# Zero products behind the units of maxima ahead of the first exponentials

## What is computed

```python
q = (x @ Wq).reshape(B, S, 2 * H, d).transpose(0, 2, 1, 3) * scaling     # 32 sub-heads, d = 4
k = (x @ Wk).reshape(B, S, 2 * H, d).transpose(0, 2, 1, 3)
v = (x @ Wv).reshape(B, S, H, 2 * d).transpose(0, 2, 1, 3)
scores = jnp.where(causal_mask, -jnp.inf, jnp.einsum('bhqd,bhkd->bhqk', q, k))
probs = jax.nn.softmax(scores, axis=-1).reshape(B, H, 2, S, S)
attn = jnp.einsum('bhqk,bhkd->bhqd', probs[:, :, 0] - lam * probs[:, :, 1], v)
attn = attn * rsqrt(mean(attn * attn) + eps) * rms_w * (1 - LAMBDA_INIT)
x = layernorm(x + attn.transpose(0, 2, 1, 3).reshape(B, S, H * 2 * d) @ Wo)
r, k = sigmoid(xr @ W_r), xk @ W_k          # xr, xk: x mixed with the token before
out = layernorm(x + r * (square(relu(k)) @ W_v))
```

## Time and profile before

| | |
|---|---|
| Median of 3 runs | 441.94 us (440.62 to 442.19) |
| Profiled execution, whole | 441.16 us |
| Its span in the profile | 439.4 us |
| TensorE busy | 395.6 us, 90% |
| VectorE busy | 397.3 us, 90% |
| ScalarE busy | 350.9 us, 80% |
| GpSimd busy | 225.2 us, 51% |
| TensorE clock granted, mean | 0.965 of full speed |

### The profile page before, as it was taken

One profiled execution on the slowest core, in us unless ns is written; L12 is line 12 of the kernel. 1 busy time (PEld: TensorE's weight loads), 2 busy tenths in 40 slices (PEclk: granted clock), 3 DMA queues, 4 the chain that ended last, 5 costly groups with the idle time before them and its releaser, 6 DMA issues.

```text
span 439.4 us, 16522 instructions
## 1 busy us (share of the span) xinstructions
PE 395.6 (90%) x5720; PEld 186.5 (42%) x5721; DVE 397.3 (90%) x565; ACT 350.9 (80%) x732; POOL 225.2 (51%) x514
## 2 busy tenths in 40 slices
PE   5846999999999999999999999999999999999882
PEld 3512444444444444444444444444444444445552
DVE  1889999999999999999999999999999999773854
ACT  2520799999999999999999999999999999787143
POOL 7300132565656565656565656565656565558412
PEclk9975599999999999999999999999999999999998
DMA  5564254321121111111111111111111110000011
GB/s 141 177 215 145 90 194 148 98 51 51 51 53 48 48 48 48 48 48 48 48 48 49 48 48 49 48 48 48 48 48 48 48 50 28 26 3 1 1 49 48
DMA packets 21390, 28.44 MB, mean 65 GB/s; under 512 B 4960, under 2 KB 9952, under 8 KB 21232
## 3 DMA queue, kind: packets, MB, share of 16 engines
q1 hardware_dynamic: 20768, 27.58, 20.9%
q10 hardware_dynamic: 592, 0.46, 0.3%
HBM read 20.39 MB, written 9.47 MB: 68 GB/s over the span
## 4 chain that ended last, share of the span: by engine, by line
PE 60%; DVE 13%; ACT 12%; issue 9%; DMA 2%; SPq 1%; POOL 1%; ACTq 1%; DVEq 0%; POOLq 0%
PE acc L677 26%; PE mx L595 13%; DVE part_max L1133 10%; ACT e_buf L1028 10%; PE ex L647 8%; PE ex L685 3%; PE mx L604 2%; PE ex L631 1%; SPq L316 1%; DMA x_tok<-in_L_attn_x 1%; PE mx L814 1%; PE mx L769 1%; PE mx L677 1%; PE ex L696 1%; POOL rs L545 1%
## 5 line engine op out<-in xcount | busy, mean ns | idle before, releaser
L1133 DVE TENSOR_REDUCE part_max<-mx 128x2 f32<-128x1024 f32 (+2 forms) x288 | 334.8, 1211 | 6.3 <-PE mx L595 2.3
L1028 ACT ACTIVATE e_buf<-ex 128x512 f32<-128x512 f32 x576 | 306.2, 601 | 36.5 <-PE ex L647 30.7
L516 POOL TENSOR_SCALAR_AFFINE_SELECT e_buf<-e_buf 128x256 f32<-128x256 f32 x256 | 100.7, 411 | 168.9 <-ACT e_buf L1028 168.7
L677 PE MATMUL acc<-e_buf,v_grp 128*32 128x256 f32 x2756 | 181.5, 352 | 4.1 <-issue 2.5
L647 PE MATMUL ex<-qe,ke 26*128 26x512 bf16 (+3 forms) x768 | 144.7, 333 | 0.7 <-ACT e_buf L1028 0.6
L595 PE MATMUL mx<-km,qm 29*128 29x128 bf16 (+3 forms) x1280 | 116.9, 270 | 12.8 <-DVE part_max L1133 10.0
L595 PEld LDWEIGHTS mx<-km,qm 26*128 26x128 bf16 (+1 forms) x1280 | 41.7, 93 | 113.8 <-DVE part_max L1133 73.5
L677 PEld LDWEIGHTS acc<-e_buf,v_grp 128*32 128x32 f32 x2756 | 64.8, 109 | 55.8 <-issue 35.5
L647 PEld LDWEIGHTS ex<-qe,ke 26*128 26x128 bf16 x768 | 45.4, 91 | 20.7 <-ACT e_buf L1028 8.2
L499 POOL TENSOR_TENSOR r_rms<-sq_eps,minus_half 128x16 f32<-128x16 f32 x15 | 43.7, 2912 | 0.1
L604 PE MATMUL mx<-mask,pick 32*128 32x128 bf16 x512 | 25.8, 220 | 0.0
(11 more groups left out here) (137 smaller groups left out, 253.6 us busy)
## 6 DMA issues: line engine op xcount, KB each, us to landing
qm<-q_rows SPq DMA_DIRECT2D x32, 128.0 KB, 2.5
km<-k_rows SPq DMA_DIRECT2D x32, 128.0 KB, 2.7
qe<-q_rows SPq DMA_DIRECT2D x32, 128.0 KB, 2.5
ke<-k_rows SPq DMA_DIRECT2D x32, 128.0 KB, 2.7
q_rows<-part_q SPq DMA_DIRECT2D x6, 256.0 KB, 3.0
k_rows<-part_k SPq DMA_DIRECT2D x6, 256.0 KB, 3.3
q_rows<-part_q SPq DMA_DIRECT2D x6, 192.0 KB
k_rows<-part_k SPq DMA_DIRECT2D x6, 192.0 KB
```

The costliest lines, as they stand in the source:

```text
L516: pool.affine_select(out=e, in_=e, compare_op=ALU.is_ge, fill=0.0, base=0, pattern=[[0, PAIR], [1, P]], channel_multiplier=-1)\
L677: last = pe.matmul(out, v, e, start=first, stop=over, skip_group_check=True)
L1028: nc.scalar.activation(e_buf[:, b, i, :], ex[:, ex_slot(b, i) % EX_BANKS, :], ACT.Exp).then_inc(s["exped"], 1)
L1133: nc.vector.tensor_reduce(target, mx_of(n, pr, m)[:].rearrange("p s (a b) -> p s a b", a=a), AX.X, ALU.max).then_inc(s["maxed"], 1)
```

## The change

`keep_busy` is defined ahead of the first loop and takes the bank as an argument. In that loop it is called with two products after the weights' transposes behind unit 4, and with two products behind each of the units 5 to 15. That makes 12 calls and 24 products of 512 columns, into bank 0 of `ex`. In unit 12 they stand ahead of the turn of the maxima, which keeps bank 2. The two calls at the end are as before. No wait, no DMA and no instruction of another engine is added, moved or removed.

```diff
+            def keep_busy(count, bank):
+                for i in range(count):
+                    pe.matmul(ex[:, bank, :], identb[:], mask_zero[:].rearrange("p c t -> p (c t)"), start=True,
+                              stop=True, skip_group_check=True)
+
...
                 if u == 4:
                     pe.wait_ge(s["rest_done"], 2 * NCH)
                     turn_weights()
+                    keep_busy(2, 0)
+                if u > 4:
+                    keep_busy(2, 0)
                 if u == NU + 3:
                     turn_maxima(0, 2)
...
-            def keep_busy(count):
-                for i in range(count):
-                    pe.matmul(ex[:, 2, :], identb[:], mask_zero[:].rearrange("p c t -> p (c t)"), start=True,
-                              stop=True, skip_group_check=True)
-
             turn_sums(NPAIR + 1, 0, last_acc)
-            keep_busy(14)
+            keep_busy(14, 2)
...
-            keep_busy(10)
+            keep_busy(10, 2)
```

## The result

The changed kernel is slower. It took 447.30 us on the median (446.79 to 448.62) against 442.06 (440.62 to 442.37) before; the ratio is 1.0129, with a 95% interval of 1.0114 to 1.0144. The forecast was 441.1 us, in a range up to 443.2. The profiled execution took 448.62 us, with a span of 446.9.

The account below looks back on a forecast made before the run. VectorE's reductions were taken to bound the kernel up to about 44 us, with TensorE's low clock lengthening pair 0 behind that. Terms: -1.71 us won in pair 0, +0.9 delay, sum -0.8, from 441.94 to 441.1 us; range 439.4 to 443.2.

Parts of the forecast that it names:

- What the low clock costs: Low clock costs nothing up to about 44 us; pair 0 at full clock would run like pair 2, winning 1.71 us.
- The high end of the gain: Pair 0 shortened to VectorE's own work of 10.75 us, winning 1.99 us.
- rival (c): Early clock rise and pair 0 at VectorE's bound: -1.9 us, 440.0 us; chance 0.12.
- When the clock rises: Clock rises at 37.0 us, within unit 9, after 7.6 us of busy TensorE; delay until then 0.9 us.
- The price of a step: At the low clock a unit and its two zero products keep TensorE 1.29 us, where VectorE needs 1.13.
- the estimated 0.11 us a load: Weight loads not hiding behind the zero products: delay about 1.1 us longer, sum an estimated +0.3 us; set aside.
- Rival (b): Zeros don't raise the clock; TensorE bounds until unit 15, 2.75 us late, nothing won: 444.7 us; chance 0.08.
- Rival (a): Clock rises, then falls in pair 0's first bursts; 0.25 us won, delay 0.9 stays: +0.65, 442.6 us; chance 0.18.
- Scatter: Allowance of 0.6 us to either side for run-to-run spread, as the three earlier runs lie 1.6 us apart.

Follow-up runs that it names:

- r9: r7 with four zero products instead of two behind units 2 and 3, and two behind the scores of pair 0's first four bursts: 439.38 us, ratio 0.9948.
- r5: Changed kernel with 14 zero products in one run behind unit 4 instead of two: 446.15 us, ratio 1.0106.
- r12: r5 with its run of 14 broken up, seven products over 128 rows and seven over rows 0 to 63 in turn: 454.64 us, ratio 1.0303.
- r13: Changed kernel with four zero products behind each unit instead of two: 444.59 us, ratio 1.0073.
- r7: Changed kernel with eight zero products while TensorE waits for the first rows, and two behind every unit from the first on: 442.09 us, ratio 1.0029.
- r4: Changed kernel with one zero product behind each unit instead of two: 442.22 us, ratio 1.0015.
- r11: Changed kernel with its 24 zero products over rows 0 to 63 alone, which the units leave free: 447.64 us, ratio 1.0125.
- r8: Kernel before the change, without its 24 zero products near the end: 444.24 us, ratio 1.0051.
- r6: r5 with all 38 products of real numbers instead of zeros: 446.01 us, ratio 1.0088.
- r1: Changed kernel with real numbers as both weights and moving data of the 24 products: median 446.49 us.
- r2: Changed kernel with real moving data in the 24 products, weights still the identity: median 444.89 us.
- r3: Changed kernel with real weights in the 24 products, zeros still streaming: median 446.92 us.
- r10: Changed kernel once more, nothing altered, for its scatter: twelve executions from 441.19 to 448.95 us, median 446.91.

## Why the prediction was wrong

**What the low clock costs, right.** Up to 44 us nothing, in pair 0 the difference to a steady pair: 1.71 us. r9 has 12.74 - 11.08 = 1.66, and its span is 437.8 against 439.4, 1.6 less. That VectorE's own work is the other bound was right (11.02 busy of 11.08), but its size was not: I took 10.75 from pair 2, where VectorE has 13 instructions, and pair 0 has 16. The high end of the gain was 12.74 - 11.02 = 1.72, not 1.99, and rival (c), built on the 10.75, asked for more than pair 0 can give.

**When the clock rises, wrong.** This is the step that failed. I took the 7.6 us of a busy TensorE ahead of the only rise in the trace for what a rise takes, and put it behind 29.34. The changed kernel's TensorE was busy for 18.3 us (31.5 to 49.8) with no rise, and the clock came up at 58.8, not at 37.0; by the mean clocks 12 of 16 executions went that way. The busy column counts a product until its end, and so covers the 0.11 us in which no columns stream; r5 and r12 have it alike and part at the clock. I had also argued that the work would be denser than that of 46.40 to 54.01. It was not: I had not looked at the starts, 0.54 apart where 0.43 is the time of the columns. Whether that is why the clock stayed low is open, as said under r13: in r7's profile the same pattern brought it up.

**The price of a step, too small.** 1.29 us was 1.50. I took the step of the zeros from the end of the kernel, where one follows another, and used it for changes between units and zeros, which have no row there. The missing 0.21 are the two changes. r4 shows that the loss is this step: with one product behind each unit it is 1.08, under VectorE's 1.13, and nearly all of the loss is gone. The Trainium skill, "TensorE: Matmul & The Clock Gate", section "Part 3: Packing small matmuls", would have given about this sum, by the estimated 0.11 us a load of the prediction: in its list of what overlaps it has a weight load wait for the running product where their rows overlap. I turned it down by the step of 0.214, which was measured on a row that was not this case. The runs don't bear the rule out as it is worded, though: a second zero product over the same rows loads beside the first (0.43 from start to start in r5), and r11's rows, which don't overlap, pay all the same.

**Rival (b), right in its mechanism, with a chance of 0.08, and mis-sized.** TensorE at 1.2 GHz became the bound until unit 15. It was to be 2.75 us late and is 5.24: the difference, 2.49, is close to the changes' 12 x 0.22 = 2.6. I had nothing won against it; 0.84 came back in pair 0. Its reason was wrong: "the zero products don't bring the clock up" is true of most executions of this pattern and not of zeros, as r5 shows. And against it I set the point that zeros hold the clock. r8 shows that they do, but to hold it and to raise it are two questions, and only the first had a row.

**Rival (a), not seen in the changed kernel's profile, seen as soon as the clock is up.** In r5, r7 and r13 it falls within the first four bursts of pair 0 (52.4, 46.6, 50.2), which is where I had put it. I had left 0.25 us won in those bursts; r5's pair 0 of 12.82 us won nothing.

**Scatter.** 0.6 us to either side was for a kernel whose clock does the same each time. With the change the executions go from 441.2 to 449.0; the mean granted clock beside each time tells to which group it belongs.

## What to carry to other kernels

Here, by the mean clocks, a filler raised the low clock in every execution where it came as one run or as four products behind each unit, and in one of four where it came as two; and it is paid at half speed until then. Put it ahead of the fall, where each product costs half and hides, and fill every thin stretch behind it as well. Before costing a filler look for a row with the same change from real product to filler, and read the starts of products and not the busy share. A step that lies below another engine's time at the upper clock can lie above it at the lower one: with 0.86 us against 1.13 the two products behind a unit cost nothing in r9, and with 1.50 they cost 5 us in the changed kernel.

## What the runs showed of the hardware

- Twice as many useless products can be faster: four behind each unit 444.6 us, two 447.3, none 442.
- No difference between products of zeros and of real numbers showed in the clock where one was tried for the other: both raised it within the run and held it behind (r5 and r6), and the counts of r1, r2 against r3, r10 can't tell them apart.
- The clock did not rise in 18.3 us in which the profile shows TensorE busy at every instant (changed kernel, 31.5 to 49.8), and it rose in r8 at 416.1, behind 0.77 us of idle time.
- Behind thin stretches the clock fell with no idle time over 1 us: at 29.5 in r7 (1.90 us busy in 3.50) and at 52.4 in r5.
- A change between products over different rows left 0.11 us without columns, at 1.2 GHz (0.54 from start to start where 0.43 is the columns) and at 2.4 GHz (0.32 where 0.21 is, 36.40 to 36.72 in r5). It did so even where the rows don't overlap (r11); a unit's and a score's products, 26 rows each, start 0.01 us apart.
- The same program fell into groups by whether and when the clock rose: 441.2, 443.4 and 446.4 to 449.0 us for the changed kernel, with mean clocks of 0.980, 0.974 and 0.952 to 0.960. What decides is open.
